# Splitting two fp32 products into hi and lo F32R halves: the first attention's output projection and the second sequence's cross-attention queries

## The reference

```
x = layernorm(x + attn(x))          # linear attention: elu + 1 features, 16 heads of 32
    q, k = elu(x Wq' + bq) + 1, elu(x Wk' + bk) + 1 ;  v = x Wv' + bv
    out = (q (k' v)) / clip(q sum(k), 1e-6)
    attn = out Wo' + bo
x = layernorm(x + xattn(x, ctx))    # softmax cross attention, 16 heads of 32
    q, k, v = x wq', ctx wk', ctx wv' ;  softmax(q k' / sqrt(32)) v wo' + bo
x = layernorm(x + moe(x))           # router: x router_w + router_b, top 2 of 8 experts,
                                    # capacity 640 rows each, gelu feed-forward of 1024
```

## Time and profile before

| | |
|---|---|
| median of 3 runs | 1981.41 us (1978.61 to 1984.81) |
| the profiled execution | 1983.6 us, span 1981.9 us |
| TensorE busy | 1894.3 us, 96% of the span |
| VectorE busy | 1218.2 us, 61% |
| ScalarE busy | 884.2 us, 45% |
| GpSimd busy | 817.0 us, 41% |
| granted TensorE clock, mean | 0.980 of 2.4 GHz |

### The profile page before, as it was taken

One profiled execution on the slowest core, in us unless ns is written; L12 is line 12 of the kernel. 1 busy time (PEld: TensorE's weight loads), 2 busy tenths in 40 slices (PEclk: granted clock), 3 DMA queues, 4 the chain that ended last, 5 costly groups with the idle time before them and its releaser, 6 DMA issues.

```text
span 1981.9 us, 26338 instructions
## 1 busy us (share of the span) xinstructions
PE 1894.3 (96%) x9904; PEld 1261.1 (64%) x9904; DVE 1218.2 (61%) x2279; ACT 884.2 (45%) x1587; POOL 817.0 (41%) x735
## 2 busy tenths in 40 slices
PE   8999999989999999999999999999969999999992
PEld 6876665667655555555445545544449999888991
DVE  6565553247678788888678778778544444444433
ACT  3212322312466666666456456456624443333431
POOL 3002201100288788888567567565022222332112
PEclk9999999989999999999999999999969999999996
DMA  7003523574668476757444434421253445454316
GB/s 272 22 1 112 186 85 138 193 206 134 157 134 185 97 180 139 168 122 157 94 112 97 103 85 109 107 62 63 75 176 91 125 131 139 104 141 111 96 18 190
DMA packets 123694, 243.53 MB, mean 123 GB/s; under 512 B 11152, under 2 KB 29344, under 8 KB 119520
## 3 DMA queue, kind: packets, MB, share of 16 engines
q1 hardware_dynamic: 108608, 185.46, 31.8%
q0 software_dynamic: 13872, 54.30, 13.8%
q10 hardware_dynamic: 1088, 2.10, 0.3%
HBM read 147.15 MB, written 62.42 MB: 106 GB/s over the span
## 4 chain that ended last, share of the span: by engine, by line
PE 83%; DVE 12%; DMA 2%; issue 1%; ACT 1%; SPq 1%; POOL 0%; ACTq 0%; POOLq 0%; DVEq 0%
PE banks L1122 36%; PE banks L1384 12%; PE banks L1291 11%; PE banks L1261 10%; PE banks L1280 8%; DVE max L1562 8%; PE banks L1312 4%; PE banks L1128 2%; DMA raw<-in_x_t 1%; DMA k_parts<-out_lo 1%; DVE stats_y L1770 0%; PE banks L1199 0%; DVE src_lo L1428 0%; DVE den_c L1581 0%; ACT src_hi L1817 0%
## 5 line engine op out<-in xcount | busy, mean ns | idle before, releaser
L1562 DVE TENSOR_REDUCE max<-banks 128x1 f32<-128x512 f32 x1024 | 627.7, 682 | 140.9 <-PE banks L1261 140.1
L2033 POOL TENSOR_TENSOR probs<-probs,probs 128x512 f32<-128x512 f32 x464 | 582.9, 1290 | 246.2 <-PE banks L1291 246.2
L1913 ACT ACTIVATE probs<-banks 128x512 f32<-128x512 f32 x1024 | 520.2, 607 | 257.7 <-PE banks L1280 257.1
L1261 PE MATMUL banks<-k_stack,q_stack 98*128 98x512 f32 x1024 | 428.7, 426 | 4.1 <-DVE max L1562 2.8
L1280 PE MATMUL banks<-q_stack,k_stack 98*128 98x512 f32 x1024 | 376.8, 398 | 2.6 <-ACT probs L1913 2.6
L1261 PEld LDWEIGHTS banks<-k_stack,q_stack 98*128 98x128 f32 x1024 | 192.1, 188 | 194.4 <-DVE max L1562 106.5
L1291 PE MATMUL banks<-probs,v_grp 128*32 128x512 f32 x2048 | 250.2, 601 | 0.0
L1280 PEld LDWEIGHTS banks<-q_stack,k_stack 98*128 98x128 f32 x1024 | 191.6, 188 | 61.7 <-ACT probs L1913 17.9
L2080 POOL DMA_INDIRECT y_rows<-eo,tok x40 | 79.8, 1996 | 216.2 <-DVE eo L1763 170.4
L1750 DVE TENSOR_TENSOR hid_lo<-hid,hid_hi 128x640 fp32r<-128x640 f32 x64 | 52.9, 826 | 143.1 <-ACT hid_hi L1978 143.1
L2044 POOL TENSOR_TENSOR x_nat<-x_nat,bxo_row 128x512 f32<-128x512 f32 x16 | 21.1, 1351 | 262.7 <-PE banks L1128 262.7
(11 more groups left out here) (228 smaller groups left out, 2696.8 us busy)
## 6 DMA issues: line engine op xcount, KB each, us to landing
k_stack<-k_parts SPq DMA_DIRECT2D x144, 256.0 KB, 5.2
w_raw<-in_L_ffn_w SPq DMA_DIRECT2D x16, 2048.0 KB, 8.3
probs<-probs POOLq DMA_DIRECT2D x31, 1024.0 KB, 10.3
q_stack<-q_parts SPq DMA_DIRECT2D x48, 256.0 KB
v_grp<-v_rows SPq DMA_DIRECT2D x48, 256.0 KB, 3.3
raw<-in_ctx_t SPq DMA_DIRECT2D x8, 1024.0 KB, 6.5
k_parts<-out_hi SPq DMA_DIRECT2D x32, 256.0 KB, 2.5
k_parts<-out_lo SPq DMA_DIRECT2D x32, 256.0 KB, 2.9
```

Of the source, the lines that this page charges most:

```text
L1261: nc.tensor.matmul(out, queries_of(t)[:, j, tile_of(k)], keys_of(t)[0:STK + SHIFT, j, mc * HALF:(mc + 1) * HALF], start=True, stop=True) \
L1562: V.reduce_max(max4[:, tiles_of(t), :, :][:, k, j, mc:mc + 1], bank(bank_of["max", t, mc, k, j]), AX.X) \
L1913: S.activation(probs_of(t, s)[:, j, :], bank(bank_of["score", t, s, j]), ACT.Exp, scale=SCALE) \
L2033: G.tensor_tensor(a[:, j, :], a[:, j, :], b[:, j, :], ALU.add).then_inc(pair_added.sem, 1)
```

## The change

`wo`, the W_o tile, is split into `wo_hi` (a new tile) and `wo_lo`, which lies where `wo` was; the four pieces are split beside the values of chunk 1. `att_t` becomes two tiles: ScalarE copies the transposed heads to the hi tile, then VectorE takes the lo tile as bank less hi, and the projection makes three products out of each. For the second sequence only (`b` = 1), W_xq and the transposed rows `x1_t` are split likewise: their hi tiles lie where W_q's parts were, so that ScalarE waits for the last query of self-attention before writing them, and the lo tiles lie over the raw ones. Its queries are made in three products. Its router logits stay fp32, and are summed over the hi and the lo tile.

```
@@ memory
+        w_parts["o"] = [put("wo_hi", [P, NC, D], F32R), Shelf(nc, wo_at)("wo_lo", [P, NC, D], F32R)]
...
-        att_t = put("att_t", [P, NG, P])
+        att_t = [put(f"att_t_{n}", [P, NG, P], F32R) for n in ("hi", "lo")]
...
+        put = Shelf(nc, loop_base)
+        w_parts["xq"] = [put("wxq_hi", [P, NC, D], F32R), Shelf(nc, wxq_at)("wxq_lo", [P, NC, D], F32R)]
+        w_raw["xq"] = wxq
+        x1_parts = [put("x1_t_hi", [P, NC, HALF], F32R), Shelf(nc, x1_t_at)("x1_t_lo", [P, NC, HALF], F32R)]
@@ the list of units
                     split_chunk(m + 1, n)
+                    if m == 1:
+                        do("split_weight", "o", n)
...
             for n in range(HT + 2):
+                if b and n >= 2:
+                    do("split_weight", "xq", n - 2)
                 stage(n)
@@ TensorE
             def project(b, n):
                 out = free_bank("project", b, n)
                 pe.wait_ge(*att_t_done[b, n])
-                pe.wait_ge(*w_in["o"]["o"])
-                accumulate(out, [(att_t[:, g, :], wo[:, g, :]) for g in range(NG)]).then_inc(projected.sem, 1)
+                pe.wait_ge(*weight_lo["o", NC - 1])
+                accumulate(out, three_passes(att_t, w_parts["o"])).then_inc(projected.sem, 1)
...
             def xq(b, h, g):
                 out = free_bank("xq", b, h, g)
                 pe.wait_ge(*x1_t_done[b, h, HT - 1])
+                if b:
+                    pe.wait_ge(*weight_lo["xq", NC - 1])
+                    accumulate(out, three_passes(columns(w_parts["xq"], tile_of(g)), x1_parts)) \
+                        .then_inc(xq_summed.sem, 1)
+                    return
...
             def x1_logits(b, h):
...
+                if b:
+                    by_column_groups(out, [(router_pad[:, c, :], x1_parts[0][:, c, :].bitcast(F32)) for c in range(NC)],
+                                     stop=False)
+                    by_column_groups(out, [(router_pad[:, c, :], x1_parts[1][:, c, :].bitcast(F32)) for c in range(NC)],
+                                     start=False).then_inc(x1_logits_summed.sem, 1)
+                    return
@@ VectorE
             def split_weight(name, c):
                 dve.wait_ge(*weight_hi[name, c])
+                if name == "xq":
+                    dve.wait_ge(*xq_summed[0, NH - 1, NG - 1])
...
+            def turn_heads(b, n):
+                dve.wait_ge(*att_t_hi[b, n])
+                V.tensor_tensor(att_t[1][:, :, :].rearrange("p g n -> p (g n)"), bank(bank_of["turn_heads", b, n]),
+                                att_t[0][:, :, :].bitcast(F32).rearrange("p g n -> p (g n)"), ALU.subtract) \
+                    .then_inc(att_t_done.sem, 1)
...
+            def turn_x1(b, h, k):
+                if b:
+                    dve.wait_ge(*x1_t_hi[b, h, k])
+                    V.tensor_tensor(x1_parts[1][:, :, tile_of(k)],
+                                    bank(bank_of["turn_x1", b, h, k]).rearrange("p (c n) -> p c n", c=NC),
+                                    x1_parts[0][:, :, tile_of(k)].bitcast(F32), ALU.subtract).then_inc(x1_t_done.sem, 1)
@@ ScalarE
             def split_weight(name, c):
...
+                if name == "xq":
+                    act.wait_ge(*queries_summed[B * NH - 1, NG - 1])
...
             def turn_x1(b, h, k):
...
+                if b:
+                    act.wait_ge(*queries_summed[B * NH - 1, NG - 1])
+                    act.wait_ge(*x1_logits_summed[(b, h - 1) if h else (b - 1, NH - 1)])
```

More of the change, by code:

```diff
@@ L224, in program @@
         w_parts["q"] = [put(f"wq_{p}", [P, NC, D], F32R) for p in ("hi", "lo")]
-        wo, wxq = put("wo", [P, NC, D]), put("wxq", [P, NC, D])
+        wo_at = put.at
+        wo = put("wo", [P, NC, D])
+        wxq_at = put.at
+        wxq = put("wxq", [P, NC, D])
+        w_parts["o"] = [put("wo_hi", [P, NC, D], F32R), Shelf(nc, wo_at)("wo_lo", [P, NC, D], F32R)]
         k_half = put("k_half", [P, HT, D])
@@ L231, in program @@
         x_nat = [put(f"x_nat{h}", [P, HT, D]) for h in range(NH)]
+        x1_t_at = put.at
         x1_t = put("x1_t", [P, NC, HALF])
@@ L394, in program @@
             "heads": lambda b, n, p: (heads_summed, heads_scaled),
-            "turn_heads": lambda b, n: (att_turned, att_t_done),
+            "turn_heads": lambda b, n: (att_turned, att_t_hi, att_t_done),
             "project": lambda b, n: (projected, row_added),
@@ L398, in program @@
             "store_x1": lambda b, h: (x1_biased, x1_out[h]),
-            "turn_x1": lambda b, h, k: (x1_turned, x1_t_done),
+            "turn_x1": lambda b, h, k: (x1_turned, x1_t_hi, x1_t_done) if b else (x1_turned, x1_t_done),
             "x1_logits": lambda b, h: (x1_logits_summed, part_hi, part_out[part_slot["x1_logits", b, h]]),
@@ L1192, in xq, with by_column_groups @@
                 pe.wait_ge(*x1_t_done[b, h, HT - 1])
+                if b:
[3 more added lines that the diff above has]
+                    return
                 pe.wait_ge(*w_in["xq"]["xq"])
                 accumulate(out, [(wxq[:, c, tile_of(g)], x1_t[:, c, :]) for c in range(NC)]).then_inc(xq_summed.sem, 1)
-            def by_column_groups(out, operands, start=True):
+            def by_column_groups(out, operands, start=True, stop=True):
                 for n, (lhsT, rhs) in enumerate(operands):
-                    done = nc.tensor.matmul(out[n * DH:(n + 1) * DH, :], lhsT, rhs, start=start, stop=True)
+                    done = nc.tensor.matmul(out[n * DH:(n + 1) * DH, :], lhsT, rhs, start=start, stop=stop)
                 return done
@@ L1792, in _ @@
                     "values": values, "queries": queries, "kv": kv_sums, "mask_kv": mask_kv, "heads": heads,
-                    "project": project, "norm1": norm1, "max": take_max, "shift_high": shift_high,
+                    "turn_heads": turn_heads, "project": project, "norm1": norm1, "turn_x1": turn_x1, "max": take_max, "shift_high": shift_high,
                     "xq": lambda *key: split_part("xq", *key), "ctx_k": lambda *key: split_part("ctx_k", *key),
@@ L1841, in turn_heads @@
                     act.wait_ge(*projected[b, n - 1] if n else projected[b - 1, NT - 1])
-                S.activation(att_t[:, :, :].rearrange("p g n -> p (g n)"), bank(bank_of["turn_heads", b, n]), ACT.Copy) \
-                    .then_inc(att_t_done.sem, 1)
+                S.activation(att_t[0][:, :, :].rearrange("p g n -> p (g n)"), bank(bank_of["turn_heads", b, n]), ACT.Copy) \
+                    .then_inc(att_t_hi.sem, 1)
             def turn_x1(b, h, k):
```

10 lines of the change are left out of this document (5 added, 5 removed).

## The result

| | before | after |
|---|---|---|
| median, us | 1981.88 (1978.61 to 1984.81, 4 runs) | 1972.71 (1969.11 to 1973.16, 4 runs) |
| profiled execution, us | 1983.6, span 1981.9 | 1973.16, span 1971.3 |
| TensorE busy | 1894.3 us | 1879.2 us |
| VectorE busy | 1218.2 us | 1237.6 us |

The medians differ by 9.2 us, where 15.1 were forecast; the ratio of the runs is 0.9946, with a 95% interval from 0.9933 to 0.9959. 1972.71 lies in the stated range of 1960 to 1975 and outside the forecast's own, 1962 to 1970. The question is where the other 6 us are.

The account below looks back on a forecast made before the run. TensorE was taken to bound the kernel from 38 to 397 us, VectorE following. 11.5 + 5.8 - 2.0 - 0.2 = 15.1 us off the median 1981.41 gave 1966.3 us; own range 1962 to 1970, stated 1960 to 1975.

Parts of the forecast that it names:

- more falls of the clock: Rival: two more clock falls cost 3.4 us, about 1970 to 1971 us; 8% together with the logits' strips case.
- projection, 16 times: Each tile's four fp32 calls, 3.44 us, become twelve F32R products, 2.72 us; 16 x 0.72 = 11.5 us saved.
- queries, 8 units: Second sequence's queries: four fp32 calls per unit become F32R products; 8 x 0.72 = 5.8 us saved.
- logits, 2 units: Second sequence's router logits: fp32 calls run on hi and lo, 1.0 us more each; 2.0 us lost, ends 1.7 and 6.9.
- lo part at the first norm: Tightest place: VectorE ends the lo part at 141.25, TensorE asks at 141.80; 0.5 us spare, no wait.
- border at 271, the wait: Context chunk border: a heads' lo part ahead of the border's src_lo makes TensorE's gap 0.2 us longer.
- the clock, two places up to the last query: Clock falls behind chunk-border gaps, 1.7 us each: one more or two fewer, +1.7 to -3.4 us.
- my own sign of being wrong: In the projection: the prediction is wrong if its twelve products take over 2.8 us.
- the figure's sum, 18.2: With the skill page's 216 ns per product, twelve take 2.59 us and the whole saving is 18.2 us instead of 15.1.
- All behind it shifted as a block: Sign: first context's end moves from 398 to near 383 us, and all later work moves with it.
- the rival that needed it, whole or in part: VectorE bounds the first sequence's row stages: whole, gain 3.8 us, 1977.6, 5%; a third of it, 1970.1, 12%.
- The rival of slower passes one after the other: Logits' second-pass strips don't overlap: 4.9 us more, about 1970 to 1971 us; 8% together with the clock falls case.

Follow-up runs that it names:

- project_twice: The changed kernel with the two moves, each projection making its twelve products twice into the same bank; 2003.40 us, one run.
- after_weights: The changed kernel where only the weight wait is parted: first context keys wait for W_k's lo parts, values for W_v's; 1973.03 us, one run.
- after_early: The changed kernel with next-chunk splits one unit earlier and first context keys waiting for W_xk's lo part alone; 1955.66 us, ratio 0.9854 to before.
- ring_swap: after_early with the two rings of PSUM banks exchanged, chunks' products in banks 4 to 7 and the rows' in 0 to 3; 1953.86 us.
- the two moves: Each next-chunk split one unit earlier, first context keys waiting for W_xk's lo part alone; on the kernel before, 1968.49 us, ratio 0.9919.

## Why the prediction was right, and where it was not

It had the direction and the mechanism: TensorE sets the time from 38 to 397 us, VectorE's added work is hidden, and what TensorE saves reaches the end where nothing waits. The size was off by 6 us. That 1972.71 lies in the stated range all the same is partly luck: its upper end was opened for VectorE as a partial bound and for more falls of the clock, and neither is what took the gain. These are the steps up to the last query; what came behind it follows under the clock. The first four measured values are from the kernels without those waits, the last three from after and before.

| step | forecast, us | measured |
|---|---|---|
| projection, 16 times | 16 x 0.72 = 11.5 | 16 x 0.62 = 9.9 |
| queries, 8 units | 8 x 0.72 = 5.8 | 8 x 0.65 = 5.2 |
| logits, 2 units | -2.0 | -1.7 |
| lo part at the first norm | 0 ("0.5 us spare, no wait") | -0.3 |
| border at 271, the wait | -0.2 | -0.07 |
| weights of the first context chunk | 0 | -1.2 |
| the clock, two places up to the last query | +3.4 to -1.7, over the whole | -1.6 and -1.6 |

- *The pace of the new products* was the mis-sized term, 2.2 us too much. I took 0.226 from one row of twelve for products that the trace before didn't have; the new ones ran at 0.233 and 0.231, so twelve took 2.80, at the very edge of my own sign of being wrong. The prediction's words "all the kernel's F32R rows at 0.226" were a misreading: the kernel's own rows in the experts stood at 0.232. The Trainium skill's figure ("TensorE: Matmul & The Clock Gate", section "Back-to-back issue gap"), some 216 ns, is still further off. The section gives it for a product by itself, and for a stream of weight loads and products some 131 ns. No row of twelve or more of the kernel's F32R products of this shape came below 0.226 on average in any run, and the figure's sum, 18.2, is above the 13.0 that the change is worth up to the last query.
- *The norm.* I looked for the wait at the tile (`att_t_lo`, rightly no wait) and not at the bank. What was pushed back on VectorE was also the divisions behind the lo part, and after two units of `turn_x1` a bank of theirs is what `project` needs. Before, they were done at 141.52 and TensorE asked at 142.52, 1.0 us spare; 0.69 of lo part and 0.66 by which VectorE's statistics there moved up less than TensorE use that up. This happens once, behind the first norm, in nine of the ten profiles of kernels with the new projection. In project_twice, where TensorE arrives later, it doesn't, which fits.
- *"All behind it shifted as a block"* failed at the first context chunk. The wait was in the earlier trace rows, 1.1 us for a weight's lo part, and I let it move with the rest, though a load stands ahead of it that takes its own time. It grew to 2.33, and the fall of the clock came with it. With the wait removed, both are gone (after_weights). The border at 398, which the forecast put near 383, came at 389.6.
- *The clock* was named with its price of 1.7 us each and an end of one more fall. Up to the last query there were two more. For the one at 271 no cause is shown: its wait grew by 0.07 us, and in after_weights a wait of 2.08 there had no fall behind it. Together with the rest the table's measured column makes 8.6 us, and the marks show 8.8 behind the last query. Behind it the clock paid back. Before, it fell behind the border at 398 and again near 427 us; after, it fell at neither place. From 383 to 440 us, before:

```profile
383.00:440.00 57.00, 49.82 (x193) 38.51 (x192) 18.06 (x29) 12.60 (x22) 0.00 (x0) 0.91 0.71 200
```

and the same work, after:

```profile
375.00:432.00 57.00, 47.78 (x206) 38.11 (x205) 20.73 (x33) 12.68 (x24) 0.00 (x0) 1.00 0.72 205
```

  By the marks this gave 1.5 us at the border and 2.1 near 427. Between them TensorE's wait for the stack of ones took 1.6 back (2.85 instead of 1.20). So the spans differ by 10.6 us, and by 11.0 when each is taken from its own second k'v sum. Over the whole execution the mean granted clock is 0.980 in both: the clock moved the marks, but of these 11.0 us it cost next to nothing. What the forecast has more than 11.0 is the pace and the longer waits. The median of before is 1.7 us under its profiled execution and that of after 0.5 under its own, which makes 9.2 of 10.4.
- *VectorE.* Its total wait for the projection fell from 29.6 to 15.1 us, 0.9 a stage, against 1.4 reckoned. The two stages shown kept 1.64 and 0.91 where 0.9 and 0.1 were forecast. It never became the bound, so the rival that needed it, whole or in part, is out. The medians near 1972 look like its partial form (1970.1), but the marks up to 225 us, where it would have had to be, lose only the pace and the 0.3 of the norm.
- *The logits' strips* overlap in the second pass. The rival of slower passes one after the other is out. Its other half, more falls of the clock, happened up to the last query and not over the whole execution.

The best kernel of these is after_early (ring_swap's single run, 1953.86 us, lies within its spread), 1955.66 us, ratio 0.9854 [0.9832, 0.9877], 29 us under the kernel before in the same rounds. Some 16 of them are the two moves', which had nothing to do with the change and left TensorE without a wait in 170 us; the change then brought its 12.8 by the medians.

## What to carry to other kernels

A saving on the engine that sets the time is worth its sum only as far as the next wait that doesn't move with it: list the waits behind it, ask of each whether a load stands ahead, and remove those first. Where an instruction is added on another engine, look at the banks that the instructions behind it give back, not only at the tile that it makes. And price a new product by the range of its like in the whole trace, here 0.226 to 0.233, not by one row.

## What the runs showed that was not expected

- The same F32R product of 128x512, with a new stationary tile each time, stood 0.227 to 0.229 us apart in most places up to 400 us and 0.231 to 0.233 in others. In the projection the one stationary tile made this difference, whatever moved against it, in whichever bank, and however many in a row (192 products in each profile, 384 in project_twice). Elsewhere the slower pace came with other tiles too.
- Gaps of 2.0 to 2.3 us on TensorE were followed by a stretch with part of the time at the 1.2 GHz level in some places and executions and not in others: at one place none behind the gap of 2.02 us before, one behind that of 2.09 after and none behind that of 2.08 in after_weights; at the last border one behind 2.02 before and none behind 2.02 after. The two that were timed cost 1.6 us each, nearly as much as the gap itself.
- A load issued 4.2 us earlier landed only 3.0 us earlier, and over fourteen profiles its time from issue to reader was 8.4 to 9.8 us, for a cause that is not shown.
